# Decoder layer on one core: VectorE takes the first maximum and one token's step ahead of the rows of the expert choice

## The reference

```python
# mixer: a state of 16x16 for each sequence and each of 16 heads, token after token
S = a * S
S = S + outer(k, b * (v - S^T k))
o = S^T q
h = x + concat(o) @ wo;  h = h + (silu(hn @ wg) * (hn @ wu)) @ wd
x1 = layernorm(x + h)
# cross-attention, 16 heads over 120 rows
p = softmax((x1 @ Wq + bq) k^T / 4);  x2 = layernorm(x1 + (p v) @ Wo + bo)
# experts: gelu(gelu(x @ W1) @ W2) @ W3 with biases, of the expert that wins
e = argmax(x2 @ Wr + br);  out = layernorm(x2 + expert_e(x2))
```

## Time and profile before

| | before |
|---|---|
| runs, median (lowest to highest) | 1966.16 us (1965.51 to 1969.77) |
| profiled execution | 1963.17 us, span 1961.2 us |
| PE busy | 1367.8 us, 70% |
| DVE busy | 1241.6 us, 63% |
| POOL busy | 1000.8 us, 51% |
| ACT busy | 755.1 us, 39% |

### The profile page before, as it was taken

How to read it: one execution, slowest core, us unless ns; L and a number is a source line. 1 busy time by engine, 2 the same in 40 slices (tenths; PEclk the granted TensorE clock), 3 DMA queues, 4 the chain that set the end, 5 groups by cost and what they waited for, 6 DMA issues and landing times. The chain is left out here.

```text
span 1961.2 us, 28586 instructions
## 1 busy us (share of the span) xinstructions
PE 1367.8 (70%) x6660; PEld 937.7 (48%) x6661; DVE 1241.6 (63%) x3264; ACT 755.1 (39%) x2416; POOL 1000.8 (51%) x1214
## 2 busy tenths in 40 slices
PE   6504558700016666667765899997499999999997
PEld 4303446400005455555554677776355555555554
DVE  4599999999989999999866143444322232232322
ACT  5422223501102566666776487886211111111110
POOL 3238888887669998888766333341111211212111
PEclk9857778955558788788877999998699999999999
DMA  4601113620030110010002111234230510511200
GB/s 126 213 6 33 44 39 96 195 99 0 0 129 27 31 32 22 22 36 25 27 26 82 52 47 45 56 122 131 65 91 17 187 38 19 176 46 61 70 16 6
DMA packets 97685, 125.41 MB, mean 64 GB/s; under 512 B 10001, under 2 KB 74952, under 8 KB 95560
## 3 DMA queue, kind: packets, MB, share of 16 engines
q1 hardware_dynamic: 60040, 97.22, 15.6%
q10 hardware_dynamic: 33136, 18.58, 3.3%
q0 software_dynamic: 4432, 8.73, 1.3%
HBM read 89.68 MB, written 35.74 MB: 64 GB/s over the span
## 5 line engine op out<-in xcount | busy, mean ns | idle before, releaser
L209 POOL TENSOR_TENSOR wt<-wt 128x1024 f32<-128x1024 f32 x128 | 304.7, 2380 | 87.6 <-DVE wt L167 86.6
L215 POOL TENSOR_TENSOR wt<-wt 128x512 f32<-128x512 f32 (+2 forms) x384 | 317.2, 826 | 30.1
L1852 PE MATMUL e_ph<-wt,e_g 128*128 x624 | 274.3, 592 | 0.0
L167 DVE SCALAR_TENSOR_TENSOR wt<-wt,scan 128x256 f32<-128x256 f32 x512 | 241.4, 471 | 0.2 <-issue 0.2
L157 DVE TENSOR_TENSOR scan<-scan,wt 128x256 f32<-128x256 f32 x512 | 219.0, 428 | 19.6 <-DVE wt L167 13.5
L148 DVE TENSOR_REDUCE scan<-wt 128x16 f32<-128x272 f32 x512 | 221.8, 433 | 0.1
L136 DVE TENSOR_TENSOR wt<-wt,scan 128x256 f32<-128x256 f32 x512 | 209.0, 408 | 5.5 <-PEq L232 5.4
L1343 ACT ACTIVATE wt<-p_pX,p_mx 128x120 f32<-128x120 f32 x512 | 176.9, 389 | 77.8 <-DVE p_mx L1130 77.6
L1475 PE MATMUL p_pm<-p_w_mix,p_oT 128*128 128x256 f32 x128 | 44.1, 504 | 221.0 <-DMA p_oT<-o 193.8
L1745 POOL TENSOR_TENSOR e_ve<-e_mv,eps 128x1 f32<-128x1 f32 x39 | 7.4, 191 | 368.9 <-DVE e_mv L1796 368.9
L1852 PEld LDWEIGHTS e_ph<-wt,e_g 128*128 128x128 f32 x624 | 115.5, 190 | 130.8 <-issue 130.8
(11 more groups left out here) (221 smaller groups left out, 2866.7 us busy)
## 6 DMA issues: line engine op xcount, KB each, us to landing
wt<-in_L_ffn_W SPq DMA_DIRECT2D x24, 1024.0 KB, 5.3
qkv<-f_st ACTq DMA_DIRECT2D x48, 256.0 KB, 2.3
p_kE<-kE SPq DMA_DIRECT2D x16, 480.0 KB, 3.7
p_vP<-vP SPq DMA_DIRECT2D x16, 480.0 KB, 4.5
e_xt<-routed ACTq DMA_DIRECT2D x39, 130.0 KB, 2.1
f_xt<-in_x SPq DMA_DIRECT2D x16, 256.0 KB, 2.8
f_raw_k<-qkv SPq DMA_DIRECT2D x4, 1024.0 KB, 5.4
f_raw_q<-qkv SPq DMA_DIRECT2D x4, 1024.0 KB, 7.8
```

The lines of the kernel that those rows point to most:

```text
L167: nc.vector.scalar_tensor_tensor(s["S"][:, h, u], s["S"][:, h, (u - 1) % R], s["gate"][:, jb, h, 1, bass.ds(c * R + u, 1)], s["outer"][:], ...
L209: nc.gpsimd.tensor_tensor(x, s["S"][:, h, z * Q:(z + 1) * Q], s["q"][:, h, now].rearrange("p t (o d) -> p t o d", o=1).to_broadcast([P, Q, ...
L215: nc.gpsimd.tensor_tensor(x[:, :, :, 0:half], x[:, :, :, 0:half], x[:, :, :, half:2 * half], ALU.add).then_inc(s["o_fold"][h], 1)
L1852: ins = nc.tensor.matmul(ph2[:], g1[:, c // (C1 // 2), c % (C1 // 2)], wt[:, bass.ds(at_b + (W2_AT + c * F2), F2)], start=(c == 0), stop=( ...
```

## The change

On VectorE, in each step, `positions(e)` moves from behind the fourth token's step (`scan(3)`) to behind the fifth (`scan(4)`), and `maximum(c, 0)`, which stood behind it, is then ahead of it.

```diff
@@ -1216,11 +1216,11 @@
                     choose(e)
                 scan(2)
                 scan(3)
-                if "e" in on:
-                    positions(e)
                 if "c" in on:
                     maximum(c, 0)
                 scan(4)
+                if "e" in on:
+                    positions(e)
                 if "c" in on:
                     maximum(c, 1)
                 scan(5)
```

## The result

| | before | after |
|---|---|---|
| median (lowest to highest) | 1966.16 us (1962.15 to 1969.77) | 1984.57 us (1979.77 to 1985.97) |
| ratio, 95% interval | | 1.0085 (1.0064 to 1.0106) |
| profiled execution | 1963.17 us, span 1961.2 us | 1984.57 us, span 1982.6 us |

A forecast was written before the change was run, and what follows sets the result against it. VectorE was taken to bound steps 5 to 7, with no engine full in the later affected steps. Terms 3.6 + 10.8 + 0.7 + 3.5 = 18.6 us longer gave 1984.8 us, range 1975 to 1995 us.

The forecast's parts named there:

- The bound and the door: Steps 5 to 7: VectorE is the bound; TensorE's `down(f, 0)` already waits for `positions`, starting 0.41 us after its first instruction.
- Start of `down(f, 0)` in steps 8 and 9: Steps 8 and 9: `down(f, 0)` starts 0.41 us behind `positions`, at 949.45 against 945.68, 3.77 us later.
- The clock: Steps 8 and 9: after the new pause TensorE starts at the low clock, 1.6 us per step, bounds 0 and 4.4.
- Steps 8 and 9, sum: Later start plus clock, 5.4 us per step with nothing hidden: 10.8 us for both, bounds 7.5 and 16.3.
- The low clock lasts: Rival, steps 8 and 9: low clock costs 4.4 us each instead of 1.6; 24.2 us longer in all; chance 0.18.
- Steps 5 to 7: The third score comes 4.04 us later, beyond its slack, so VectorE waits: 2 x 0.29 + 3.04 = 3.6 us longer.
- Step 10: No down product; the second maximum comes 0.71 us later and ScalarE waits for it: 0.7 us, from 0 up.
- Steps 16 to 20: `down(f, 0)` starts one maximum later, 0.7 us per step: 3.5 us for five steps, at least 0.
- The scores' side wins: Rival, all twelve steps: earlier maximum gains 0.71 us each, 8.5 us faster; chance 0.07 together with a cover for everything.

The follow-up runs named there:

- e4: After's order, but the first two instructions of `positions` (read of `places`, running total) stay ahead of the first maximum; 1.0008 of before, 1.6 us longer.
- e5: After's order, with `places` in PSUM buffer `pq`, so the values' product waits for `positions` instead of the down product; 1.0017 of before, 3.3 us longer.
- e1: Kernel before with the new order in steps 8 to 10 alone; 1.0058 of before, 11.4 us longer.
- e9: After plus 7 unread matmuls in steps 8 and 9, ahead of TensorE's wait for `positions`; 1.0049 of before, 9.6 us longer.
- e8: Kernel before, with GpSimd reading out the first part of the scan ahead of the first variances in steps under 16 tokens; 0.9986 of before, 2.8 us shorter.
- e10: e8 plus 55 unread matmuls in four TensorE waits of steps 8 to 10; 0.9965 of before, 6.9 us shorter, one execution of 7820.84 us left out.
- e2: Kernel before with the new order in steps 5 to 7 alone; 1.0013 of before, 2.6 us longer.
- e3: Kernel before with the new order in steps 16 to 21 alone; 1.0017 of before, 3.3 us longer.
- e7: After plus 13 unread matmuls in steps 8 and 9, ahead of TensorE's wait for `positions`; 1.0085 of before, 16.7 us longer.

## Why the prediction was right, point by point

**The bound and the door.** Right. The ten of the twelve steps that have a down product (5 to 9 and 16 to 20) lose because `down(f, 0)` stands behind the read of `places`. Shown from both sides: e4 moves the read back and leaves the rest, e5 takes away what made it wait and leaves VectorE's order; they give back 15.1 and 13.4 of 16.7 us.

**Start of `down(f, 0)` in steps 8 and 9.** Forecast 3.77 us later, measured 3.18 in step 8. The maximum came earlier against the logits (8.02 instead of 8.49 us), and the product started 0.28 us behind `positions` and not 0.41. In step 9 it was 1.97, or 3.7 without the faster queries, as in step 9 of e1 (3.65) and e9 (3.62).

**The clock.** Forecast 1.6 us a step, measured 2.4 and 2.3. This term of the sum was mis-sized, and the reason for it was wrong: I read 1.6 and 4.4 us as belonging to steps 5 and 7. The time from `down(f, 0)` to the third score, at full clock 4.86 us, moves about between executions where that part of the order is the same:

| | step 5 | step 6 | step 7 | step 8 | step 9 |
|---|---|---|---|---|---|
| before | 6.48 | 6.48 | 9.24 | 4.86 | 4.86 |
| e1 (5 to 7 as before) | 5.84 | 9.23 | 6.53 | 9.26 | 7.52 |
| e8 (5 to 9 as before) | 5.82 | 9.25 | 6.52 | 4.87 | 4.87 |
| e10 (5 to 9 as before) | 6.52 | 5.83 | 9.25 | 4.86 | 4.87 |
| after | 6.84 | 7.13 | 7.36 | 7.28 | 7.15 |

The 4.4 us fell on step 7, 6 or, in e1, 8. Not every number above 4.86 is clock, though. Timeline of e8, step 5 (5.82 us):

```profile
770.98 3.02 PE L1499 MATMUL p_py<-p_wd,p_prod 128*128 128x256 f32 x12 [1.42 <-DVE scan L1193]
773.93 1.96 PE L1543 MATMUL p_pq<-p_prT,p_vP 120*32 120x128 f32 x64
776.80 1.08 PE L1521 MATMUL p_pX<-p_kE,p_qT 32*128 32x240 f32 x8 [0.92 <-ACT wt L1346]
```

Both products ran at full clock here, and the third score then waited 0.92 us for ScalarE's exponentials. The 5.84 and 5.83 us of the table are the same. Nor is it always 4.86 us where TensorE did not pause: step 8 of e2 has 6.10 and of e3 5.72, both at full clock, because the 64 small records of the values' product came with gaps.

What goes with the clock is the pause. In six profiles (before, e1, e3, e4, e8, e10) `down(f, 0)` waits in steps 5 to 7 as in before, 18 pauses in all. The down product kept the full clock behind the five shortest pauses (1.42 to 1.57 us; 3.02 us for its twelve records). It lost 1.6 us or so behind seven (1.60 to 2.18 us; 4.66 to 4.71), and behind the six longest (2.33 to 2.48 us) it and the values' product were slow to the end, 4.4 us in all. Longer pauses didn't cost more: after's 5.20 to 6.49 us cost 2.0 to 2.5. This is an ordering seen in rows; what makes one pause longer than another, and whether that also decides the clock, isn't shown.

The Trainium skill ("TensorE: Matmul & The Clock Gate", What's actually happening) says that how many matmuls run slow differs from run to run. The table bears it out, and it was the rule to go by, not the place.

**Steps 8 and 9, sum.** Forecast 10.8, in the profile 9.9, and e1 has 11.4 for steps 8 to 10. Start and clock erred in opposite directions, so the sum was better than its terms. That is luck, and so is that the forecast of 1984.8 us meets the median of 1984.57: e1's profile has 15.1 us for the same two steps. "The low clock lasts" holds now and then (e1, step 8), not as the rule.

**Steps 5 to 7.** Forecast 3.6 us as 0.29 + 0.29 + 3.04, measured 0.47 + 0.77 + 1.05 = 2.3 (e2: 2.6). The mechanism was right: VectorE's waits before the third maximum, 0.40, 0.70 and 0.97 us, are the loss to 0.2 us. The split was wrong for the reason above.

**Step 10.** Forecast 0.7, measured 0.23 in after and 0.40 in e1. Executions in which this step's order is as before differ by more (+0.97 in e2, -0.38 in e3), so neither number shows a loss.

**Steps 16 to 20.** Forecast 0.7 each, measured 0.69, 0.68, 0.68, 0.53 and 0.54 (3.1 instead of 3.5; e3: 3.3).

**Not foreseen.** 2.27 us in step 11 of the profiled execution, where neither kernel differs. There the mix product waited 2.27 us for a transfer instead of 1.39, and its eight records took 3.58 us instead of 1.99, at the low clock. e7 has the same (2.50 and 3.60 us), e9 and e1 ran it at full clock. So it doesn't come with the changed order each time, nor with the clock of steps 8 and 9. What decides it is open.

**The scores' side wins.** Refuted everywhere: the maximum was 0.7 us earlier in its order and gained nothing, since in steps 8, 9 and 16 to 20 it waits for the scores in either order (3.50 us in step 8 and 5.70 in step 16 of after). In steps 5 to 7 it did come 0.7 us earlier (10.83 instead of 11.55 us behind the logits of step 5), and the third maximum waited instead.

## What to carry to other kernels

When a piece of work moves behind others on one engine, ask first which buffer it reads and who is waiting to overwrite it: here the user of its result had room (GpSimd was idle 9.57 us in step 8, and e4's late writes cost next to nothing), and the engine that wanted the buffer had 2.2 us in step 8 (2.63 us from the first instruction of `positions` to the down product, of which 0.41 is needed) for a move of 5.5. Where such a wait can't be avoided, give the small result a buffer that is wanted later (e5), or split the read from the rest (e4). A wait of TensorE that is on the path costs its own length and, after it, often the clock: price that as a range over several executions, not from the row at one place, and look whether what stands behind it is slow or waits.

## What the runs showed of the hardware that I had not expected

- A float32 matmul of 128x256 is two records of 0.23 us at full clock (26 for 13, 14 for 7). Whoever takes the 0.23 us for each matmul in the code gets half the time.
- A pause of 0.64 us of TensorE kept the full clock, and so did five of 1.42 to 1.57 us; thirteen of 1.60 to 2.48 us lost it; pauses of 3.5 us lost it for the down product in e1 and in after, yet the queries behind the same 3.52 us ran at full clock in step 9 of after (1.97 us), slower in before (2.55) and slower still in e8 (3.75).
- Unread matmuls in TensorE's waits made the program shorter: 7.1 us between after and e9 (medians; some 2 to 12 by the intervals), and e10 is 6.9 us below before, of which e8 alone has 2.8.
